# Last pair's first back attention: row sums taken by matmuls with a 0/1 pattern and the mix divided behind them

## The chip, the cores and the metric

The kernel runs on one core of one Trainium2 chip. The metric is the device time of one execution in microseconds (us). The kernel before takes 651.56 us, the median of three runs (649.15 to 652.43).

## The reference, cut to what matters

Eight sequences of 128 rows and width 128 go through four rounds of "x = x + attention(norm(x), context); x = x + feed-forward(norm(x))". The context of a sequence has 120 rows. The change touches the attention and the feed-forward of round 1 (named L1X and L1F in the kernel):

```
Qh, Kh, Vh = heads of x @ W_Q + b_Q, ctx @ W_K + b_K, ctx @ W_V + b_V     # 16 heads of width 8
scores     = einsum(Qh, Kh) / sqrt(8)  + causal, padded keys and rows at -inf
importances = nan_to_num(softmax(scores))
attn       = einsum('bhqk,bhkd->bhqd', importances, Vh)
x          = x + heads_joined(attn) @ W_O + b_O                            # L1X

Wq = sign(W / g) * min(round(|W / g|), 1),   g = mean(|W|) + 1e-6          # ternary weights of L1F
x  = x + layernorm(gelu(norm(x) @ Wq_fc.T)) @ Wq_proj.T                    # L1F
```

A softmax divides each row of exponentials by its sum. The quotient can be taken before the product with the values or after it: the sum belongs to one head and one query row.

## The kernel before

Two sequences make a pair, and the two sequences of a pair are the two lanes, 0 and 1; there are four pairs. A pair first goes through round 0 (the "early" steps, stream `p`, and the "front" steps, stream `f`, with 32 expert tiles of 8 products each) and then, lane by lane, through the six layers L1X to L3F (the "back" steps, streams `0` and `1`). Each engine writes its steps as four generators, and a table of letters, `ORDER`, says for each engine from which stream the next step is taken. An engine runs its instructions strictly in that order and waits at each for semaphores. The front of the next pair overlaps the back of the pair before it. The back of the last pair has no front beside it any more: from about 550 us on only its two lanes are left, and TensorE gets spare transposes of the identity (L688) in the slots where the table puts an `f`. At the beginning 14 warm steps of two dummy products (`keep_busy`) are spread in the same way.

All data is float32. One product of a 128x128 stationary tile (`lhsT`) is two MATMUL instructions in the trace; a transpose is one. TensorE writes three PSUM banks for each lane (`bank[lane][0..2]`, printed as bank10, bank11, bank12 for lane 1).

L1X of one lane goes like this. Four products give the scores of four heads each (128 rows by 4 times 120 columns), into three banks, the fourth into the first bank again. DVE reads each bank with the mask added (`take_scores`, recorded at L1502) and takes the row maxima (L1805). ACT computes the exponential head by head; `accum_out` makes each activation also deliver its row sum, by an extra instruction, ACTIVATION_READ_ACCUMULATOR (L1190). DVE inverts four sums at a time (`invert_sums`, L1816), POOL multiplies the four heads by them (`normalise_probs`, L1397), TensorE transposes the four heads (L785), and ACT or DVE copies the transposed bank to `wide_a` (`take_transposed`, or in the last pair `move_transposed` for the first `MOVED` = 2 banks, L1811). The mix then is 16 products, one for each head: a stationary tile of 32 columns of `v`, whose columns outside the head's own eight are zero, and 128 moving columns. Head 4j+c adds to the output partitions 32j to 32j+31:

```python
for c in range(4):
    for j in range(4):
        h = 4 * j + c
        last = mm(bank[lane][2][32 * j:32 * j + 32, 0:S], v[lane][0:K, 32 * h:32 * h + 32], ...)
```

So four instructions in a row go to four different groups of output partitions. ACT copies the mix (`mixT_ready`), TensorE multiplies it with `wo`, DVE adds it to x, and `turn_x` (L774) transposes the new x for L1F. In the program's order the lane whose L1X is first in the last pair is lane 1.

The ternary weights of L1F are made once, at the beginning, by DVE (`late_setup`, part of stream `0`): three small operations on the thresholds, then three operations of 512 columns for each of the two matrices, all in one step.

Of the kernel before, what the change touches and what calls it, by code (L numbers as in the profile page):

```python
# [23 lines left out]
MOVED = 2  # L24
# [23 lines left out]
    "PE": "pfppffpp00pp00fffffppppppppffffffffffffppff0fffppfpp00p00ffpfpf0pffpffppffffpffpfpfp0ffpfffpfffpfffp"  # L48
          "fffffpp0p10p01pfpff10fp10fff000f0p000f0010fp00f00f0p10ff001p10pff101101000f0pf0p1f1100101f0p11f10f11"
          "p0f001p10ff0ff10f11111111001ff1010110100fff1pfff1100p110101pfp1ff110f0ffffp0ffpff0pffpff11f01f1p01f1"  # L50
          "pf01ff1pf1f11011000fp011p00p11p100f1100p110f1p0101ff0p01ff10p000000001f1010111101000101fff10f01p1101"
          "0100ff01100ff1001011p1f110pf0110p1f01f01pff1000f100001f00p0ff00f001110f01100110f111f011f01f10001010f"
          "110100f01f10111110100101ff0f0f010f010111f10f01f1f11f11f1f110f110010110100f1ff1fffff1fff011ff11110011"
          "1001010001010010010000111000fff11101000000000101000001f111101f11100010001101111ff1110001101fffff",
    "Activation": "ppppp000ppppp0pppppp0ppppp00f0000pppf0ppfpffpfpfpfpppp00ppppp0p10ppp010f00011000p10f000001p10000fp10"
                  "0pp11f100100f001fp1111f0p1f11pp01p0110000001111101100001100000p1p0111p1111111ppp0101ff1111p000pf00pp"
                  "ff0f11pffp111111001110000p10p11p01p1101000p111pp10001p010000101111000p001000111000001110pp0001011f01"
                  "11111p11p0011p001f10000001101000pf00110001110101f0p111f11f001ff1100100110111110100010000000001111011"
                  "1100111111111101001100111100110101111110001000011100000111000100000110010010010111000010110101110101"
                  "1111010",  # L60
    "DVE": "ppppp0ppp0pppppppppppfffpfpfppppppfff00pppppfpfffppffffppffpffppppfpfffpppp0ffffpppppfffpppfffpppfpf"
           "ppf0ff1pff0f000f10fpff00011ffff101100000f1pp01pff000ffp0pp0p110p000ffffff0011101p001pppp11000000f11f"
           "f011f0pf11111f11f0ppfppppf01f10101101p001f01pppf00ffff1fffffpff00ppffp000f00fff111111011ffp1111111ff"
           "p11pffffp00f11p0000ff0111ppp1pp011p01ppp000f001ff10000f110p00f1111000p100101ppp0f0ppfpf11ff111101ff0"
           "0000010ffff1p0f111011110010000pf1f0011f111010pfff000011f0pp0001101101ff010f10010f0111000111ff1f11f00"
           "00000f0ff1110111111f11f000000fff1111111f10ff11001111110110110000100001111100000100100110100100000000"
           "01110000111110000001111110111100000011111110101",
    "Pool": "pppp1000f0fp111100000011f000011p1001110011000001011110101111fff1000p00001111111p01001101100011000011"
            "1000f10110111ff0000010011110000110111010010011010001011011111fff110110111000100111000010101000100011"
            "1011",  # L70
    "SP": "pppfffffffpffffffffffffffffpffffpffffffffffffffffffffpffffffffffffffffff0ppfff1ffffffffffffffpffffff"
          "fff0fffffffff1f1ff0pfffffffffffffffffpfffffffffff10ffff01f1001ffff",
}


def width(members):
    return sum(n for _, n in members)


def build(nc, x_in, ctx_in, q_mask, k_mask, pair_mask, packs, experts, gates_of, out):  # L80
    with ExitStack() as stack:
# [301 lines left out]
        with nc.Block() as block:  # L383
# [103 lines left out]
            def _(pe):  # L487
# [1600 lines left out]
```

## Time and profile before

| What | us |
| --- | --- |
| median of 3 runs | 651.56 |
| the profiled execution's own time | 650.43 |
| its span (first to last instruction) | 648.8 |
| TensorE (PE) busy | 629.2 |
| VectorE (DVE) busy | 504.2 |
| ScalarE (ACT) busy | 367.1 |
| GpSimd (POOL) busy | 212.4 |

The page also cuts the span into 40 slices: PE stands at 9 tenths or more nearly everywhere, with 8 tenths in the first slice and in several of the last seven. DMA moves little after about 550 us. The chain that ended last runs through PE for 88% of the span and through ACT for 5%. All times in the rows are counted from the start of the span. In a row of a timeline the first number is the start, the second the length, "xN" the instructions merged into the row, and the brackets give idle time before it and what ended it.

### The profile page before, as it was taken

The page shows a single profiled execution, that of the slowest core. Times are in us where ns is not written, and L with a number is a line of the kernel's source. Part 1 is how long each engine was busy: PE and PEld are TensorE (multiplying, and loading weights), DVE is VectorE, ACT ScalarE, POOL GpSimd, SP SyncE. Part 2 cuts the span into 40 slices and gives each one's busy share as a digit, 9 for nine tenths or more (in the row PEclk, how much of TensorE's full clock was granted, in tenths as well). Part 3 has the DMA queues.
Part 4 walks back from the last instruction along what each step waited for, and adds up shares of the span by engine and source line. Part 5 has one row for each costly group of instructions (what it writes and reads, how often), then busy time and mean ns, then how long its engine had stood idle before and what let it go on. Part 6 is the DMA issues. An engine that isn't in the chain of part 4 may idle for free.

```text
span 648.8 us, 14778 instructions
## 1 busy us (share of the span) xinstructions
PE 629.2 (97%) x5582; PEld 580.7 (90%) x5582; DVE 504.2 (78%) x1352; ACT 367.1 (57%) x1255; POOL 212.4 (33%) x252
## 2 busy tenths in 40 slices
PE   8999999899999999999999999999999999898889
PEld 7899999788999999999889999988899999567878
DVE  3886677898696868887987889879778586775776
ACT  3442132377465747354665677568666563866774
POOL 1000004465031512424531444154343531643040
DMA  8986969887614734899525318451552720000000
GB/s 339 413 285 217 308 215 330 295 281 255 238 38 131 260 123 134 293 302 349 169 90 175 103 47 289 162 193 35 162 202 98 268 74 5 6 2 1 2 2 9
DMA packets 37078, 111.93 MB, mean 173 GB/s; under 512 B 8976, under 2 KB 11664, under 8 KB 36496
## 3 DMA queue, kind: packets, MB, share of 16 engines
q1 hardware_dynamic: 37008, 110.99, 49.7%
q8 instruction: 44, 0.72, 0.4%
q14 instruction: 26, 0.21, 0.1%
HBM read 109.93 MB, written 1.05 MB: 171 GB/s over the span
## 4 chain that ended last, share of the span: by engine, by line
PE 88%; ACT 5%; DVE 4%; DMA 2%; issue 1%; POOL 0%; SPq 0%; DVEq 0%; ACTq 0%
PE bank L489 37%; PE e_bank L489 37%; PE p_bank L489 5%; PE bank L785 4%; ACT wide_b L1190 3%; DMA gated<-gates_of 2%; PE bank L774 1%; DVE gated L1499 1%; PE p_bank L594 1%; ACT wide_a L1045 1%; PE e_bank L688 1%; PE bank L1023 1%; PE bank L867 1%; DVE f_route L1499 0%; PE bank L627 0%
## 5 line engine op out<-in xcount | busy, mean ns | idle before, releaser
L489 PE MATMUL e_bank<-weights,gated 128*128 128x128 f32 x1984 | 235.2, 275 | 0.7 <-DVE gated L1499 0.7
L489 PEld LDWEIGHTS e_bank<-weights,gated 128*128 128x128 f32 x1984 | 228.2, 192 | 3.9 <-issue 1.6
L1190 ACT ACTIVATE wide_b<-wide_b,max_neg 128x120 f32<-128x120 f32 x272 | 103.4, 385 | 10.0 <-DVE max_neg L1805 6.2
L1397 POOL TENSOR_TENSOR wide_b<-wide_b,row_inv 128x480 f32<-128x480 f32 x64 | 70.9, 1114 | 115.1 <-DVE row_inv L1816 115.0
L1499 DVE TENSOR_TENSOR gated<-gated,f_v 128x1024 f32<-128x1024 f32 x64 | 77.2, 1234 | 9.1 <-DMA gated<-gates_of 5.0
L1389 POOL TENSOR_TENSOR rstd<-var_eps,w_const 128x1 f32<-128x1 f32 (+1 forms) x48 | 33.7, 702 | 152.9 <-DVE var_eps L1495 152.8
L1499 DVE TENSOR_TENSOR gated<-gated,f_xnT 128x1024 f32<-128x1024 f32 x60 | 77.8, 1333 | 2.8 <-DMA gated<-gates_of 2.6
L1045 ACT ACTIVATE wide_a<-bank 120x512 f32<-120x512 f32 (+5 forms) x103 | 53.5, 539 | 46.1 <-PE bank L489 19.0
L1190 ACT ACTIVATION_READ_ACCUMULATOR wide_b<-wide_b,max_neg 128x1 f32 x272 | 52.1, 191 | 0.0
L1805 DVE TENSOR_REDUCE max_neg<-wide_b 128x4 f32<-128x480 f32 x64 | 41.8, 653 | 2.2
L1045 ACT ACTIVATE f_v<-e_bank 128x512 f32<-128x512 f32 x32 | 19.2, 600 | 36.1 <-PE e_bank L489 36.1
L785 PE MATMUL bank<-w_const,wide_b 128*120 128x128 f32 x256 | 37.1, 275 | 2.4 <-POOL wide_b L1397 2.1
L1282 ACT ACTIVATE wide_a<-bank,w_L2f 128x128 f32<-128x128 f32 x128 | 34.7, 417 | 4.7 <-PE bank L489 4.7
L785 PEld LDWEIGHTS bank<-w_const,wide_b 128*120 128x120 f32 x256 | 28.8, 138 | 6.9 <-issue 4.9
L1045 ACT ACTIVATE wide_b<-bank 128x480 f32<-128x480 f32 (+2 forms) x40 | 20.6, 520 | 22.1 <-PE bank L489 22.1
L1343 POOL TENSOR_TENSOR f_rstd<-f_var_eps,w_const 128x2 f32<-128x2 f32 x8 | 8.4, 1045 | 73.0 <-DVE f_var_eps L1495 65.9
L489 PE MATMUL bank<-w_L2f,wide_a 128*128 128x128 f32 x256 | 31.4, 276 | 0.0
L489 PE MATMUL bank<-xnT,w_L2f 128*128 128x128 f32 x256 | 31.2, 276 | 0.0
L1095 ACT ACTIVATE f_b<-p_bank,f_max_neg 128x128 f32<-128x128 f32 x56 | 19.8, 371 | 19.6 <-DVE f_max_neg L1565 19.6
L489 PEld LDWEIGHTS bank<-w_L2f,wide_a 128*128 128x128 f32 x256 | 29.9, 192 | 0.4
L489 PEld LDWEIGHTS bank<-xnT,w_L2f 128*128 128x128 f32 x256 | 29.9, 193 | 0.0
L1502 DVE SCALAR_TENSOR_TENSOR wide_b<-bank,rstd,w_L3x 128x480 f32<-128x480 f32 x32 | 22.6, 706 | 7.6 <-PE bank L489 7.5
(274 smaller groups left out, 1236.8 us busy)
## 6 DMA issues: line engine op xcount, KB each, us to landing
gated<-gates_of SPq DMA_DIRECT2D x124, 512.0 KB, 5.6
weights<-in_experts SPq DMA_DIRECT2D x64, 512.0 KB, 6.1
w_L2f<-in_L2f SPq DMA_DIRECT2D x1, 2124.0 KB, 16.8
w_L3x<-in_L3x SPq DMA_DIRECT2D x1, 2108.0 KB, 11.9
w_L3f<-in_L3f SPq DMA_DIRECT2D x1, 1128.0 KB, 14.1
wide_b<-in_raw0f SPq DMA_DIRECT2D x1, 1024.0 KB, 7.5
w_L1f<-in_L1f SPq DMA_DIRECT2D x1, 516.0 KB, 8.0
x_next<-in_x SPq DMA_DIRECT2D x4, 128.0 KB, 4.6
```

What stands on the lines that cost most here:

```text
L489: return nc.tensor.matmul(o, lhsT, rhs, start=first, stop=last)
L785: last = nc.tensor.transpose(bank[lane][(1, 2, 0, 1)[i]][0:K, 128 * c:128 * c + 128], wide_b[lane][:, K * h:K * h + K], ident)
L1045: return nc.scalar.activation(o, i, ACT.Identity, bias=bias, scale=scale)
L1095: last = nc.scalar.activation(f_b[lane][:, 128 * h:128 * h + 128], unit_bank(pair, lane)[:, 128 * c:128 * c + 128], ACT.Exp, bias=f_max_ne ...
L1190: last = nc.scalar.activation(p, p, ACT.Exp, bias=max_neg[lane][:, h:h + 1], accum_out=row_sum[lane][:, h:h + 1])
L1282: last = nc.scalar.activation(wide_a[lane][:, at:at + 128], bank[lane][(1, 0, 2, 1)[i]][:, 128 * c:128 * c + 128], ACT.Gelu, bias=part["L2 ...
L1343: return nc.gpsimd.tensor_tensor(to[:, :], rows[:, :], part["const", "minus_half"][:, 0:2], ALU.pow)
L1389: nc.gpsimd.tensor_tensor(rstd[lane][:, cols], var_eps[lane][:, cols], part["const", "minus_half"][:, 0:cols.stop - cols.start], ALU.pow)\
L1397: nc.gpsimd.tensor_tensor(p3, p3, row_inv[lane][:, 4 * i:4 * i + 4].unsqueeze(2).broadcast_to([128, 4, K]), ALU.mult).then_inc(probs_norme ...
L1499: return nc.vector.tensor_tensor(o, a, c, op)
L1502: return nc.vector.scalar_tensor_tensor(o, a, scalar, c, op0, op1)
L1805: nc.vector.tensor_reduce(max_neg[lane][:, 4 * i:4 * i + 4], s3, AX.X, ALU.max, negate=True)\
```

## The change

In the last pair only, L1X no longer sums, inverts and multiplies ahead of the transposes. The exponentials run without `accum_out`. The transposes wait for the exponentials alone. For each group j of four heads, TensorE does four products with a 0/1 pattern (`head_cols`: 32 columns, ones in the head's eight) into columns 128 to 255 of the mix's bank, which gives every output partition the row sum of its head, and then the four products with `v`. The four groups are four steps; the third and the fourth wait for their own transposed bank. DVE then takes the reciprocal of 128x128 sums out of PSUM and multiplies the mix by it, which replaces ACT's copy. DVE moves one transposed bank (`MOVED_L1X` = 1) in place of two in L1X; ACT takes the other three. The step that makes the ternary weights is split into three, by two `yield`s. The first warm step of TensorE waits for the zeros it multiplies, as the early step did. And `ORDER` is new for all five engines.

```diff
-MOVED = 2
+MOVED_L1X, MOVED_L3X = 1, 2
...
 ORDER = {
-    "PE": "pfppffpp00pp00fffffppppppppffffffffffffppff0fffppfpp00p00ffpfpf0pffpffppffffpffpfpfp0ffpfffpfffpfffp"
...
+    "PE": "pfpffpffpfp0pp000fffpffpfpppppp0fffffffffpfpfffppfpp00p0ff0pfpfppffff0pffpffpf0fpfpfpffpffpffffpffff"
...
                 def front_steps():
+                    pe.wait_ge(idle_filled, 1)
                     for _ in range(WARM):
...
-                        pe.wait_ge(probs_normed[lane], probs_normed.upto(layer, i + 1, pair))
+                        if layer == L1X and pair == PAIRS - 1:
+                            pe.wait_ge(probs_ready[lane], probs_ready.upto(L1X, i + 1, pair))
+                        else:
+                            pe.wait_ge(probs_normed[lane], normed_upto(probs_normed, layer, i + 1, pair))
...
                     wait_turned(pe, lane, L1X, 1, pair)
-                    wait_turned(pe, lane, L1X, 3, pair)
-                    for c in range(4):
+                    if pair == PAIRS - 1:
                         for j in range(4):
-                            h = 4 * j + c
-                            last = mm(bank[lane][2][32 * j:32 * j + 32, 0:S], v[lane][0:K, 32 * h:32 * h + 32],
-                                      wide_a[lane][0:K, 128 * h:128 * h + 128], c == 0, c == 3)
+                            if j >= 2:
+                                wait_turned(pe, lane, L1X, j, pair)
+                            r = slice(32 * j, 32 * j + 32)
+                            for c in range(4):
+                                h = 4 * j + c
+                                mm(bank[lane][2][r, S:2 * S], part["const", "head_cols"][0:K, 32 * c:32 * c + 32],
+                                   wide_a[lane][0:K, 128 * h:128 * h + 128], c == 0, c == 3)
+                            for c in range(4):
+                                h = 4 * j + c
+                                last = mm(bank[lane][2][r, 0:S], v[lane][0:K, 32 * h:32 * h + 32],
+                                          wide_a[lane][0:K, 128 * h:128 * h + 128], c == 0, c == 3)
+                            if j < 3:
+                                yield
...
-                            last = nc.scalar.activation(p, p, ACT.Exp, bias=max_neg[lane][:, h:h + 1],
-                                                        accum_out=row_sum[lane][:, h:h + 1])
+                            if layer == L1X and pair == PAIRS - 1:
+                                last = nc.scalar.activation(p, p, ACT.Exp, bias=max_neg[lane][:, h:h + 1])
...
                     def normalise_probs(layer):
+                        if layer == L1X and pair == PAIRS - 1:
+                            return
...
                     link(ts(threshold[:, 0:2], threshold[:, 0:2], 0.5, None, ALU.mult))
+                    yield
...
+                        if late_sums:
+                            dve.wait_ge(mix_psum[lane], mix_psum.upto(L1X, 1, pair))
+                            link(nc.vector.reciprocal(wide_b[lane][:, S:2 * S], bank[lane][2][:, S:2 * S]))
+                            tt(wide_b[lane][:, 0:S], bank[lane][2][:, 0:S], wide_b[lane][:, S:2 * S], ALU.mult)\
+                                .then_inc(mixT_ready[lane], 1)
```

What the new table does is seen in the order of an engine's instructions. First TensorE, at the mix of lane 1 in the last pair; bank00 to bank02 are lane 0's banks, L688 is a spare transpose. Before:

```order
L785 MATMUL bank12<-w_const,wide_b_1 120x128 x4
L688 MATMUL e_bank<-w_const 128x128 x9
L489 MATMUL bank00<-wide_a_0,small_0 128x480
L785 MATMUL bank10<-w_const,wide_b_1 120x128 x4
L785 MATMUL bank11<-w_const,wide_b_1 120x128 x4
L688 MATMUL e_bank<-w_const 128x128 x6
L489 MATMUL bank12<-wide_a_1,v_1 32x128 x16
```

and in the changed kernel, down to the first of the four groups:

```order
L501 MATMUL bank02<-wide_a_0,small_0 128x480
L801 MATMUL bank12<-w_const,wide_b_1 120x128 x4
L801 MATMUL bank10<-w_const,wide_b_1 120x128 x4
L801 MATMUL bank11<-w_const,wide_b_1 120x128 x4
L501 MATMUL bank00<-wide_a_0,small_0 128x480
L501 MATMUL bank12<-wide_a_1,w_const 32x128 x4
L501 MATMUL bank12<-wide_a_1,v_1 32x128 x4
```

The spares between the transposes are gone, lane 0's fourth scores product stands directly ahead of the mix, and the last two rows stand four times in a row with nothing between them; lane 0's mix has the same form, right behind lane 1's product with the ternary `proj`.

Second DVE, around the normalised mix of lane 1 in the last pair; the rows with mask1_0 read lane 0's scores, the row with x_mid_bias1_1 makes lane 1's new x. Before:

```order
L1502 SCALAR_TENSOR_TENSOR wide_b_0<-bank02,mask1_0 128x480
L1805 TENSOR_REDUCE max_neg_0<-wide_b_0 128x4
L1816 RECIPROCAL row_inv_0<-row_sum_0 128x4
L1502 SCALAR_TENSOR_TENSOR wide_b_0<-bank00,mask1_0 128x480
L1502 SCALAR_TENSOR_TENSOR x_1<-bank10,row_ok_1,x_mid_bias1_1 128x128
```

and in the changed kernel:

```order
L1540 SCALAR_TENSOR_TENSOR wide_b_0<-bank02,mask1_0 128x480
L1845 TENSOR_REDUCE max_neg_0<-wide_b_0 128x4
L1879 RECIPROCAL wide_b_1<-bank12 128x128
L1537 TENSOR_TENSOR wide_b_1<-bank12,wide_b_1 128x128
L1540 SCALAR_TENSOR_TENSOR wide_b_0<-bank00,mask1_0 128x480
```

Lane 0's fourth bank of scores now stands behind the reciprocal, which waits for lane 1's whole mix.

Third DVE at the beginning, around the thresholds of the ternary weights; f_xn is the normalised x of the first pair. Before:

```order
L1495 TENSOR_SCALAR f_var_eps<-f_mean_var 128x2
L1496 TENSOR_SCALAR f_xn<-f_x0,f_mean_var,f_rstd 128x128 x2
L1496 TENSOR_SCALAR threshold<-bank00 128x2
L1495 TENSOR_SCALAR threshold<-threshold 128x2 x2
L1495 TENSOR_SCALAR wide_a_1<-w_L1f,threshold 128x512
```

and in the changed kernel:

```order
L1533 TENSOR_SCALAR f_var_eps<-f_mean_var 128x2
L1534 TENSOR_SCALAR threshold<-bank00 128x2
L1533 TENSOR_SCALAR threshold<-threshold 128x2 x2
L1534 TENSOR_SCALAR f_xn<-f_x0,f_mean_var,f_rstd 128x128 x2
L1533 TENSOR_SCALAR wide_a_1<-w_L1f,threshold 128x512
```

The three threshold operations moved ahead of f_xn, which waits for POOL. On TensorE the four products of w_L1f with wide_a_1 moved from behind the second expert tile to ahead of the first gate transposes, and eight of the twelve dummies that stood there moved to earlier slots.

## Rows read from the trace of the kernel before

**Rows 1.** Busy time by stretch: us, then PE, PEld, DVE, ACT, POOL; PEclk, DMA.

```profile
500.00:525.00 25.00, 25.00 (x252) 23.83 (x253) 16.68 (x36) 15.10 (x62) 10.47 (x12) 1.00 0.60 201
550.00:575.00 25.00, 21.86 (x191) 15.57 (x191) 18.00 (x47) 20.93 (x86) 16.21 (x18) 1.00 0.03 7
575.00:600.00 25.00, 21.67 (x151) 17.49 (x150) 15.85 (x72) 14.85 (x45) 7.94 (x10) 1.00 0.00 1
```

**Rows 2.** What PE waited for, 550 to 650 us: total, times, longest.

```profile
PE bank L785 <- POOL wide_b L1397: 2.1, 3, 1.6
```

**Rows 3.** PE timeline of L1X and L1F in the last pair.

```profile
561.66 0.97 PE L489 MATMUL bank<-wide_a,small 128*128 128x480 f32 x2
564.69 1.08 PE L489 MATMUL bank<-wide_a,v 120*32 120x128 f32 x32
565.70 0.48 PE L489 MATMUL bank<-w_L2x,ctx_back 128*120 128x128 f32 x2
567.52 0.27 PE L774 MATMUL bank<-w_const,x 128*128 128x128 f32 x1
573.31 1.08 PE L489 MATMUL bank<-wide_a,v 120*32 120x128 f32 x32
574.32 0.33 PE L879 MATMUL bank<-w_const,small 120*128 120x120 f32 x1
576.21 0.27 PE L774 MATMUL bank<-w_const,x 128*128 128x128 f32 x1
```

**Rows 4.** PE by tile shape, whole span: count, busy us, mean ns of one.

```profile
L489 PE MATMUL bank<-wide_a,v 120*32 120x128 f32 x256 | 8.5, 275 | 0.1
L489 PE MATMUL bank<-wide_a,v 120*64 120x128 f32 x256 | 17.5, 279 | 1.0 <-ACT wide_a L1045 0.7 <-DVE wide_a L1811 0.3
L489 PE MATMUL e_bank<-weights,gated 128*128 128x128 f32 x1984 | 235.2, 275 | 0.7 <-DVE gated L1499 0.7
```

**Rows 5.** ACT timeline in the last pair's L1X and L2F.

```profile
554.37 0.40 ACT L1190 ACTIVATE wide_b<-wide_b,max_neg 128x120 f32<-128x120 f32 x1 [0.66 <-DVE max_neg L1805]
554.77 0.38 ACT L1190 ACTIVATE wide_b<-wide_b,max_neg 128x120 f32<-128x120 f32 x1
563.46 1.08 ACT L1045 ACTIVATE wide_a<-bank 120x512 f32<-120x512 f32 x2
596.92 6.30 ACT L1282 ACTIVATE wide_a<-bank,w_L2f 128x128 f32<-128x128 f32 x24 [0.43 <-PE bank L489]
```

**Rows 6.** DVE groups by shape: count, busy us, mean ns of one.

```profile
L1603 DVE RECIPROCAL f_group<-f_group 128x16 f32<-128x16 f32 x8 | 2.0, 253 | 0.3
L1599 DVE RECIPROCAL f_group<-f_group 128x32 f32<-128x32 f32 x8 | 2.8, 353 | 0.3
L1499 DVE TENSOR_TENSOR x<-bank,x 128x128 f32<-128x128 f32 x16 | 4.6, 286 | 8.3 <-PE bank L489 8.0
```

**Rows 7.** DVE timeline: two banks of lane 1's scores in the last pair.

```profile
553.00 0.66 DVE L1502 SCALAR_TENSOR_TENSOR wide_b<-bank,mask 128x480 f32<-128x480 f32 x1 [0.89 <-PE bank L489]
554.26 0.65 DVE L1502 SCALAR_TENSOR_TENSOR wide_b<-bank,mask 128x480 f32<-128x480 f32 x1
```

**Rows 8.** DVE timeline at the beginning.

```profile
16.99 0.60 DVE L1496 TENSOR_SCALAR f_xn<-f_x,f_mean_var,f_rstd 128x128 f32<-128x128 f32 x2 [0.83 <-POOL f_rstd L1343]
17.51 0.15 DVE L1496 TENSOR_SCALAR threshold<-bank 128x2 f32<-128x2 f32 x1
18.10 0.48 DVE L1495 TENSOR_SCALAR wide_a<-w_L1f,threshold 128x512 f32<-128x512 f32 x1
27.59 0.29 DVE L1499 TENSOR_TENSOR f_gate<-f_route 128x128 f32<-128x128 f32 x1
```

**Rows 9.** PE timeline at the beginning.

```profile
25.57 2.84 PE L489 MATMUL e_bank<-small 128*128 128x128 f32 x24
28.25 1.47 PE L627 MATMUL bank<-w_const,f_gate 128*128 128x128 f32 x12
37.14 1.06 PE L489 MATMUL bank<-w_L1f,wide_a 128*128 128x128 f32 x8
```

More of the change, by code:

```diff
@@ L55 @@
[L55 to L67, printed above, removed]
@@ L819, in back_lane @@
                     wait_turned(pe, lane, L1X, 1, pair)
-                    wait_turned(pe, lane, L1X, 3, pair)
-                    for c in range(4):
+                    if pair == PAIRS - 1:
                         for j in range(4):
-                            h = 4 * j + c
-                            last = mm(bank[lane][2][32 * j:32 * j + 32, 0:S], v[lane][0:K, 32 * h:32 * h + 32],
-                                      wide_a[lane][0:K, 128 * h:128 * h + 128], c == 0, c == 3)
+                            if j >= 2:
[11 more added lines that the diff above has]
+                                yield
+                    else:
+                        wait_turned(pe, lane, L1X, 3, pair)
+                        for c in range(4):
+                            for j in range(4):
+                                h = 4 * j + c
+                                last = mm(bank[lane][2][32 * j:32 * j + 32, 0:S], v[lane][0:K, 32 * h:32 * h + 32],
+                                          wide_a[lane][0:K, 128 * h:128 * h + 128], c == 0, c == 3)
                     last.then_inc(mix_psum[lane], 1)
@@ L903, in back_lane @@
                     yield
-                    wait_turned(pe, lane, L2X, MOVED if pair == PAIRS - 1 else 0, pair)
+                    wait_turned(pe, lane, L2X, 0, pair)
                     for h in range(H2X):
@@ L1204, in softmax_banks @@
                                 yield
-                            if n >= behind and (pair < PAIRS - 1 or n - behind >= MOVED):
+                            if n >= behind and n - behind >= moved(layer, pair):
                                 take_transposed(layer, n - behind, lane)
@@ L1218, in back_lane @@
                     yield from softmax_banks(L1X, 2)
-                    act.wait_ge(mix_psum[lane], mix_psum.upto(L1X, 1, pair))
-                    copy(wide_b[lane][:, 0:S], bank[lane][2][:, 0:S]).then_inc(mixT_ready[lane], 1)
-                    yield
+                    if pair < PAIRS - 1:
+                        act.wait_ge(mix_psum[lane], mix_psum.upto(L1X, 1, pair))
+                        copy(wide_b[lane][:, 0:S], bank[lane][2][:, 0:S]).then_inc(mixT_ready[lane], 1)
+                        yield
                     act.wait_ge(kv_psum[lane], kv_psum.upto(L2X, 1, pair))
@@ L1727, in late_setup @@
                             link(last)
+                            yield
                     last.then_inc(setup_computed, 1)
@@ L1823, in softmax_banks @@
                             yield
-                        invert_sums(layer, 0, lane)
-                        yield
+                        late_sums = layer == L1X and pair == PAIRS - 1
+                        if not late_sums:
+                            invert_sums(layer, 0, lane)
+                            yield
                         take_scores(layer, 3, lane, scale, added)
@@ L1828, in softmax_banks @@
                         for i in range(1, 4):
-                            invert_sums(layer, i, lane)
-                            yield
-                            if pair == PAIRS - 1 and i <= MOVED:
+                            if not late_sums:
+                                invert_sums(layer, i, lane)
+                                yield
+                            if i <= moved(layer, pair):
                                 move_transposed(layer, i - 1, lane)
                                 yield
+                        if late_sums:
[3 more added lines that the diff above has]
+                                .then_inc(mixT_ready[lane], 1)
+                            yield
                     dve.wait_ge(kv_psum[lane], kv_psum.upto(L1X, 2, pair))
```

56 lines of the change are left out of this document (40 added, 16 removed).

## The prediction, made before the changed kernel ran

> **What bounds the kernel now.** I read the busy times by stretch first. In the middle of the span PE has no idle time (25.00 of 25.00 us from 500 to 525), so there only PE's own work counts. From 550 to 600, where the last pair's lanes run alone, PE is busy 21.86 and 21.67 of 25 and idles 6.5 us [rows 1]. The waits of PE in that stretch name POOL's normalised exponentials with 2.1 us in three waits [rows 2]; that is the wait the change removes. The PE timeline then shows the stage itself: lane 1's mix starts at 564.69, lane 1's new x is turned at 567.52, lane 0's mix starts at 573.31, lane 0's new x is turned at 576.21 [rows 3]. ACT runs exponentials nearly without a gap before the first mix, 0.40 us from one start to the next [rows 5]. So the stage is a chain over ACT, POOL and PE's order, and PE has some room in it.
>
> **The mix, the dear part.** The change adds 16 products for each lane and moves the order from "four output groups in turn" to "one group eight times". Three kinds of PE rows tell what that costs. Instructions with a stationary tile of 32 columns, issued in turn to four groups, take 8.5 us for 256, 33.2 ns each. Those of 64 columns, in turn to two groups, take 17.5/256 = 68.4 ns. Those over the full width take 235.2/1984 = 118.5 ns. The length of one alone is the same for all, 275 to 279 ns [rows 4]. The price goes as one over the number of groups that take turns: four instructions run beside each other, then two, then one. In the new order eight products, 16 instructions, in a row go to one group, so nothing can run beside them, and the next group's eight follow in program order. I cost them at 118.5 ns: 64 instructions for a lane, 7.6 us, where 32 now take 1.01 us (564.69 to 565.70, and 573.31 to 574.32) [rows 3]. The lower bound is 33.2 ns, 2.1 us, if the array overlaps them all the same; the upper is 4 x 33.2 = 133 or 2 x 68.4 = 137 ns, 8.8 us. I take the full-width row: it is the only one in which one group takes everything. The Trainium skill ("TensorE: Matmul & The Clock Gate", section "Measured speedup vs the span model") reports 2.38 times for three column groups, less than the ratio here (118.5/33.2 = 3.6 for four). By that page, scaled to four groups (3.2, an estimate), the 64 instructions would take 1.01 x 2 x 3.2 = 6.4 us, and the sum below would be 2.4 us lower.
>
> **Lane 1, term by term.** (a) The start of the mix. Gone from the chain are POOL's multiplication and, in ACT, the accumulator reads. DVE reads a bank of scores every 1.26 us (553.00, 554.26) [rows 7]. Without the read I cost an exponential at 0.26 us, from the 24 activations without a sum in 6.30 us [rows 5], so ACT's 16 take 4.2 us. The new order makes ACT copy two things of lane 0 first, which PE delivers only behind lane 1's fourth scores product; I put the first exponential 1.5 us after 554.37. Then 4.2, a copy of 0.2, and the first transposed bank, 0.54 (half of 1.08) [rows 5]: 560.8. Lane 0's fourth scores product, 0.8 us long, ends at about 560.5 by DVE's pace. The mix starts at about 561.0, 3.7 us earlier than now. The third and fourth bank are copied by 562, while the first two groups still run, so their separate waits cost nothing; nor do they gain anything. (b) The mix ends 7.6 us later in place of 1.0: +6.6. (c) Between its end and the turn of x are now 567.52 - 565.70 = 1.8 us. ACT's copy goes; DVE's reciprocal of 128x128 comes. Rows of 16 and 32 columns take 253 and 353 ns, 6.25 ns a column, so 353 + 96 x 6.25 = 0.95 us for 128; the multiplication is a row of 0.29 [rows 6]. Bounds: 0.35 (the longest row there is) and 1.4 (the same out of PSUM at half the speed). Behind the wait on DVE stands lane 0's fourth bank of scores, 1.26 us, and only then lane 1's new x; the product with `wo` hides under it. Landing and waits 0.3, 0.95 + 0.29, 1.26, the new x 0.35: 3.2, so +1.4. The Trainium skill ("VectorE: DVE Perf Modes", section "First, the fixed hardware budget") says that the reciprocal divides iteratively with a repeat count of 8. At 0.96 GHz that makes 1.07 us plus the fixed part, an estimate; by it the sum would be 0.3 higher for both lanes, and the rows' slope of 6.25 ns agrees better with 6 cycles. Together lane 1's x is turned at -3.7 + 6.6 + 1.4 = +4.3.
>
> **Lane 0.** From there to lane 0's mix PE's order is the same before and after, 5.8 us (567.52 to 573.31) [rows 3]. All four banks of lane 0 are ready by then, so again the whole 7.6 lies on PE's path: +6.6. From its end to the turn of lane 0's x: 2.3 in place of 1.9, +0.4. Lane 0 is late by 4.3 + 6.6 + 0.4 = 11.3. Lane 1 doesn't escape: its keys and its next x stand behind lane 0's mix on PE. What comes later has the same work in nearly the same order, and the two lanes wait for each other there; I let 0.8 be absorbed in PE's idle time of 575 to 600 [rows 1]. The tail: +10.5. Bounds: about 0 at 33 ns (below), +13 at 137 ns. The 32 inverted sums, the 8 multiplications on POOL and ACT's other savings are in (a) and count for nothing elsewhere.
>
> **The beginning.** The thresholds move into DVE's 0.83 us wait for POOL: 18.10 - 17.51 = 0.59 us off the chain to the first gates (27.59) [rows 8]. PE's dummies end at 28.25, 0.37 after f_gate is written at 27.88; eight of them move away. And eight instructions, 0.95 us, move from 37.14, where PE is full, to ahead of the gates, where only dummies ran [rows 9]. At best 0.6 + 0.4 + 0.9 = 1.9 us; nothing if the DMA-fed tiles behind can't keep up. I take 1.5, since PE has hardly any idle time from then to 550 that could eat it. The ternary step's division alone, and the wait for the zeros, cost nothing: DVE's and PE's rows around them keep their order. The rest of the table I cost at 0, within 1 us either way; two more table loads of ACT fall where PE is full.
>
> **The sum.** 650.4 (the profiled execution) + 10.5 - 1.5 = 659.4. That execution is 1.1 below the median of the runs, 651.56, so the median should be between 659.4 and 660.5; I say 660.
>
> **Rivals.** First, the groups run side by side after all. For it: the array is seen to run four of these tiles at once, and neighbouring groups touch at their borders. Against: the ladder of 33, 68 and 118 ns, which has no step left below one group. The mix then takes 64 x 33.2 = 2.1 us: lane 1 is -3.7 + 1.1 + 1.4 = -1.2, lane 0 +0.3, the tail about 0, and the beginning's 1.5 stays: 649, not slower. It decides from 48 ns an instruction down, where two mixes of 3.1 us use up what (a) and the beginning give. Second, half the added 13 us finds room: PE idles 6.5 us from 550 to 600 and ran spare transposes there besides. Then the tail is +5.3 and the time 654.2. Against it: the mix is one unbroken row in PE's order, and the other lane's work stands behind it. Third, PE's clock falls while the array is a quarter filled for 7.6 us. Granted was 1.00 in every stretch, which is 2.4 GHz [rows 1]; at the lower level, 1.2 GHz, the two mixes take 15 us more: 675.
>
> **How the numbers follow.** Less than 0.5% (3.3 us: under 648.3 faster, over 654.8 slower) can't be told from no change here. Forecast 0.75, all slower, with a range of its own of 655 to 665. Side by side 0.12, split between faster (0.07) and the same (0.05). Half hidden 0.10, 0.07 the same, 0.02 slower, 0.01 faster. Clock 0.03, slower. Faster 0.08, same 0.12, slower 0.80. The range 651 to 665 leaves out the first rival and the third.
>
> **What would show it.** Right: groups of 32-column products in the last pair with about 118 ns an instruction, 7 to 8 us for each lane without a gap; a DVE reciprocal of about 1 us in two places; lane 0's x turned near 586 (576.2 + 11.3 - 1.5); the first gate transposes near 27.4; and the busy time of PE up by 10 to 13 us. Wrong: the mix in 2 to 3 us; or the mix as long as said, but the turn of lane 0's x late by less than 6 us; or a granted clock under 1.

## The result, and the profile after

The changed kernel takes 661.03 us, the median of 4 runs (659.83 to 661.50), where the kernel before takes 651.99 beside it (649.15 to 653.44): a ratio of 1.0144, 95% interval 1.0125 to 1.0162. It is slower by 1.4%. Of the four executions the profiled one (659.83) shows a mean granted clock of 1.000 and the other three (660.71 to 661.50) 0.997, so sums over stages below go by traces and not by this median. The page of the changed kernel gives the span and PE's work; the span was 648.8 and PE 629.2 before.

```profile
span 658.2 us, 14857 instructions
...
PE 639.1 (97%) x5646; PEld 590.6 (90%) x5646; DVE 502.2 (76%) x1346; ACT 370.8 (56%) x1225; POOL 198.0 (30%) x244
```

PE is busy for 9.9 us longer, and the span is 9.4 us longer. The last two stretches of [rows 1], with the columns as there:

```profile
550.00:575.00 25.00, 20.97 (x146) 14.32 (x145) 15.71 (x35) 16.12 (x48) 8.74 (x11) 1.00 0.03 9
575.00:600.00 25.00, 22.82 (x180) 19.09 (x179) 13.01 (x53) 11.99 (x33) 4.14 (x7) 1.00 0.01 2
```

The granted clock is 1.00 in both. From 550 to 600 PE is busy for 43.8 us, about as before (43.5), but it got less far: the turn of lane 0's x, at 576.21 in [rows 3], comes at 585.54. PE's timeline, with the rows that answer to [rows 3] and the border between the first two groups of lane 1's mix in full:

```profile
549.91 0.27 PE L787 MATMUL bank<-w_const,xn_mid 128*128 128x128 f32 x1
...
560.56 0.62 PE L801 MATMUL bank<-w_const,wide_b 128*120 128x128 f32 x4 [0.29 <-ACT wide_b L1223]
561.02 0.97 PE L501 MATMUL bank<-wide_a,small 128*128 128x480 f32 x2
561.92 1.06 PE L501 MATMUL bank<-wide_a,w_const 120*32 120x128 f32 x8
562.82 0.71 PE L501 MATMUL bank<-wide_a,v 120*32 120x128 f32 x5
563.26 0.30 PE L501 MATMUL bank<-wide_a,w_const 120*32 120x128 f32 x1
563.37 0.27 PE L501 MATMUL bank<-wide_a,v 120*32 120x128 f32 x1
563.40 0.27 PE L501 MATMUL bank<-wide_a,w_const 120*32 120x128 f32 x1
563.48 0.27 PE L501 MATMUL bank<-wide_a,v 120*32 120x128 f32 x1
563.51 0.27 PE L501 MATMUL bank<-wide_a,w_const 120*32 120x128 f32 x1
563.59 0.27 PE L501 MATMUL bank<-wide_a,v 120*32 120x128 f32 x1
563.62 0.71 PE L501 MATMUL bank<-wide_a,w_const 120*32 120x128 f32 x5
...
567.81 0.48 PE L501 MATMUL bank<-w_L2x,ctx_back 128*120 128x128 f32 x2
...
570.76 0.33 PE L787 MATMUL bank<-w_const,x 128*128 128x128 f32 x1 [0.16 <-DVE x L1540]
...
576.96 1.06 PE L501 MATMUL bank<-wide_a,w_const 120*32 120x128 f32 x8
...
582.85 0.32 PE L911 MATMUL bank<-w_const,small 120*128 120x120 f32 x1
...
585.54 0.27 PE L787 MATMUL bank<-w_const,x 128*128 128x128 f32 x1
```

Read the starts. Lane 1's mix runs from 561.92 to 567.81 and lane 0's from 576.96 to 582.85, 5.89 us each for 64 instructions, 92 ns on average. Within a group eight start in 0.90 us (561.92 to 562.82), 112 ns apart: one alone, as forecast. The ninth, with which the group passes from its sums to its values and so to other columns of the bank, starts 0.11 us behind the eighth like the others, so it is not the adding into one place that keeps them apart. Whether it is the product itself or the load of its stationary tile stays open: PEld's timeline has the group's first eight loads end to end as well, in 0.79 us (561.92 to 562.71). At the border to another group it is different. The last three of the old group (`v`) and the first three of the new one (`w_const`) start in turn, six in 0.36 us (563.26 to 563.62). Three such borders in each mix give back 1.3 us of the 64 x 0.112 = 7.2. PE by tile shape shows the sum, to compare with [rows 4]: the 320 instructions of 32 columns now take 23.1 us, where 256 took 8.5.

```profile
L501 PE MATMUL bank<-wide_a,v 120*32 120x128 f32 x256 | 14.6, 275 | 0.0
L501 PE MATMUL bank<-wide_a,w_const 120*32 120x128 f32 x64 | 8.5, 276 | 0.0
```

DVE's timeline behind lane 1's mix, which answers to [rows 6] and to the order shown for DVE:

```profile
567.92 0.96 DVE L1879 RECIPROCAL wide_b<-bank 128x128 f32<-128x128 f32 x1 [4.72 <-PE bank L501]
568.91 0.29 DVE L1537 TENSOR_TENSOR wide_b<-bank,wide_b 128x128 f32<-128x128 f32 x1
569.12 0.65 DVE L1540 SCALAR_TENSOR_TENSOR wide_b<-bank,mask 128x480 f32<-128x480 f32 x1
...
570.37 0.34 DVE L1540 SCALAR_TENSOR_TENSOR x<-bank,row_ok,x_mid_bias 128x128 f32<-128x128 f32 x1
```

The reciprocal of 128x128 takes 0.96 us (0.95 forecast), and DVE waited 4.72 us for it. ACT's first eight exponentials of lane 1, to compare with [rows 5], and further on the four of lane 0's fourth bank with the two copies behind them; then, from the kernel before, the last of the 24 exponentials that start in one run at 554.37:

```profile
555.48 2.39 ACT L1223 ACTIVATE wide_b<-wide_b,max_neg 128x120 f32<-128x120 f32 x8
...
570.49 1.26 ACT L1223 ACTIVATE wide_b<-wide_b,max_neg 128x120 f32<-128x120 f32 x4 [1.24 <-DVE max_neg L1845]
571.65 0.58 ACT L1077 ACTIVATE v<-bank 120x512 f32<-120x512 f32 x1
572.12 0.26 ACT L1077 ACTIVATE xnT<-bank 128x128 f32<-128x128 f32 x1
```

```profile
563.09 0.39 ACT L1190 ACTIVATE wide_b<-wide_b,max_neg 128x120 f32<-128x120 f32 x1
```

Without the sum eight take 2.39 us, and what stands behind them starts 2.29 us after the first (557.77): one every 0.29 us. With it the first two start 0.40 us apart [rows 5], and over all 24 it is one every 0.38 us (8.72 us for 23 steps).

At the beginning the change did gain: the first gate transposes start at 27.96 (28.25 in [rows 9]), and the products of `w_L1f` behind them at 43.05, where they started at 44.23. But PE then waits in a place where it hardly did before. PE's row behind that wait, and DVE's timeline that explains it:

```profile
102.12 1.16 PE L501 MATMUL p_bank<-f_xnT,f_b 128*128 128x128 f32 x8 [1.68 <-ACT f_b L1127]
```

```profile
95.62 1.22 DVE L1537 TENSOR_TENSOR gated<-gated,f_v 128x1024 f32<-128x1024 f32 x1 [1.43 <-DMA gated<-gates_of]
98.69 1.23 DVE L1537 TENSOR_TENSOR gated<-gated,f_v 128x1024 f32<-128x1024 f32 x1 [1.85 <-DMA gated<-gates_of]
99.84 0.68 DVE L1603 TENSOR_REDUCE f_max_neg<-p_bank 128x4 f32<-128x512 f32 x1
```

The row maxima at 99.84, for which ACT's `f_b` and with it PE wait, stand behind multiplications that wait for gates from a DMA (1.43 and 1.85 us). Before, the same row stood two tiles earlier:

```profile
96.67 0.69 DVE L1565 TENSOR_REDUCE f_max_neg<-p_bank 128x4 f32<-128x512 f32 x1 [0.42 <-PE p_bank L489]
```

Of the gain 0.23 us is left when the last pair begins (549.91 in place of 550.14). That is one execution of each: the traces of later versions whose program is the same up to there, and whose clock stayed at 1.00, begin the last pair between 548.70 and 549.66, and one with the old beginning begins it at 552.63.

### The profile page after: what moved, and what is told of

Read it like the earlier page. It is cut to its first block, busy times and chain, and to the rows that moved or that the text cites. A ratio compares the mean times of both kernels' runs of the same rounds, so it can differ in the third digit from the quotient of the medians.

```text
span 658.2 us, 14857 instructions
## 1 busy us (share of the span) xinstructions
PE 639.1 (97%) x5646; PEld 590.6 (90%) x5646; DVE 502.2 (76%) x1346; ACT 370.8 (56%) x1225; POOL 198.0 (30%) x244
## 4 chain that ended last, share of the span: by engine, by line
PE 88%; ACT 5%; DMA 3%; DVE 3%; issue 1%; POOL 0%; SPq 0%; DVEq 0%
PE bank L501 38%; PE e_bank L501 35%; PE p_bank L501 5%; PE bank L801 4%; DMA gated<-gates_of 3%; ACT wide_b L1225 2%; PE bank L787 1%; PE e_bank L701 1%; ACT wide_b L1223 1%; PE p_bank L606 1%; PE bank L899 1%; DVE gated L1537 1%; DVE wide_b L1540 1%; PE bank L1055 1%; DVE max_neg L1845 1%
## 5 line engine op out<-in xcount | busy, mean ns | idle before, releaser
L1225 ACT ACTIVATE wide_b<-wide_b,max_neg 128x120 f32<-128x120 f32 x240 | 91.7, 388 | 16.0 <-DVE max_neg L1845 15.2
L1435 POOL TENSOR_TENSOR wide_b<-wide_b,row_inv 128x480 f32<-128x480 f32 x56 | 60.3, 1087 | 97.6 <-DVE row_inv L1856 97.6
L1425 POOL TENSOR_TENSOR rstd<-var_eps,w_const 128x1 f32<-128x1 f32 (+1 forms) x48 | 29.6, 618 | 171.0 <-DVE var_eps L1533 170.5
L1537 DVE TENSOR_TENSOR gated<-gated,f_xnT 128x1024 f32<-128x1024 f32 x60 | 75.5, 1298 | 6.3 <-DMA gated<-gates_of 6.1
L1225 ACT ACTIVATION_READ_ACCUMULATOR wide_b<-wide_b,max_neg 128x1 f32 x240 | 46.3, 193 | 0.0
L501 PE MATMUL bank<-wide_a,v 120*32 120x128 f32 (+1 forms) x512 | 32.1, 277 | 0.4 <-DVE wide_a L1851 0.3
L501 PEld LDWEIGHTS bank<-wide_a,v 120*32 120x32 f32 (+1 forms) x512 | 25.6, 123 | 5.0 <-issue 2.8
```

Of the source, the lines that this page charges most:

```text
L501: return nc.tensor.matmul(o, lhsT, rhs, start=first, stop=last)
L1225: last = nc.scalar.activation(p, p, ACT.Exp, bias=max_neg[lane][:, h:h + 1], accum_out=row_sum[lane][:, h:h + 1])
L1425: nc.gpsimd.tensor_tensor(rstd[lane][:, cols], var_eps[lane][:, cols], part["const", "minus_half"][:, 0:cols.stop - cols.start], ALU.pow)\
L1435: nc.gpsimd.tensor_tensor(p3, p3, row_inv[lane][:, 4 * i:4 * i + 4].unsqueeze(2).broadcast_to([128, 4, K]), ALU.mult).then_inc(probs_norme ...
L1537: return nc.vector.tensor_tensor(o, a, c, op)
```

## The experiments

The question was whether the added 9.4 us are the order of the mix, the division behind it, or the table, and where the beginning's gain went. Each ratio is against the kernel before, run beside it on the same chip. "The stage" is the time from the turn of lane 1's xn_mid to the turn of lane 0's x on PE: 26.07 us before (550.14 to 576.21), 35.63 in the changed kernel.

| Version | us | before | ratio, 95% interval |
| --- | --- | --- | --- |
| mix in turn | 651.97 | 651.22 | 1.0010 (0.9996 to 1.0025) |
| two groups in turn | 653.87 | 651.22 | 1.0042 (1.0028 to 1.0057) |
| kernel before, one group | 654.38 | 651.22 | 1.0047 (1.0031 to 1.0063) |
| bank first | 658.42 | 651.22 | 1.0116 (1.0093 to 1.0139) |
| turn and bank | 651.23 | 651.05 | 1.0003 (0.9983 to 1.0023) |
| and maxima earlier | 650.02 | 651.05 | 0.9971 (0.9956 to 0.9987) |
| turn, bank, sums first | 650.59 | 651.05 | 0.9996 (0.9978 to 1.0014) |
| beginning only | 650.57 | 651.05 | 0.9985 (0.9967 to 1.0003) |
| everything | 648.35 | 650.89 | 0.9958 (0.9945 to 0.9971) |
| beginning, maxima, old attention | 647.80 | 650.89 | 0.9950 (0.9934 to 0.9966) |

**The mix in turn over four groups.** In the last pair, in the changed kernel (shortened; the waits for the third and fourth transposed bank now stand ahead of all 64 instructions):

```diff
-    for j in range(4):
-        for c in range(4):  (pattern into group j)
-        for c in range(4):  (v into group j)
+    for c in range(4):
+        for j in range(4):  (pattern into group j)
+    for c in range(4):
+        for j in range(4):  (v into group j)
```

> The changed kernel with the same 64 instructions for a lane's mix, but in turn over the four output groups (first the 16 products with the pattern, then the 16 with v). Theory, the price of one group at a time: the mix falls from 5.89 us to 64 x 33.2 ns = 2.1 us, 3.8 us less for each lane, and both lie on the path: the turn of lane 0's x comes 7.6 us earlier (578.0), the span is 650.6 and the time 653.4. Rival one, the division behind the mix and its place in DVE's order are the loss: the mix is as short, but the turn of lane 0's x gains under 2 us and the time stays at 659 or more. Rival two, lane 1's mix lies beside other work: only lane 0's 3.8 us come back, time 657.

PE's timeline:

```profile
549.52 0.27 PE L787 MATMUL bank<-w_const,xn_mid 128*128 128x128 f32 x1
...
561.60 1.08 PE L501 MATMUL bank<-wide_a,w_const 120*32 120x128 f32 x32
...
563.49 0.48 PE L501 MATMUL bank<-w_L2x,ctx_back 128*120 128x128 f32 x2
...
573.12 1.08 PE L501 MATMUL bank<-wide_a,w_const 120*32 120x128 f32 x32 [0.40 <-ACT wide_a L1078]
...
575.01 0.32 PE L912 MATMUL bank<-w_const,small 120*128 120x120 f32 x1
...
577.72 0.27 PE L787 MATMUL bank<-w_const,x 128*128 128x128 f32 x1
```

Each mix takes 1.89 us (561.60 to 563.49), 29.5 ns an instruction, and the stage 28.20. The span is 650.4. The mix's order alone carries nearly the whole loss, and both lanes' mixes lie on the path: 8.0 us of mix came off, 7.4 of stage. Both rivals fall. The time is 1.4 us below the 653.4 expected, which was counted from the median of 661.03; counted from the profiled 659.83 it would have been 652.2.

**Two groups in turn.** The same edit, with groups 0 and 1 first and then 2 and 3.

> The changed kernel with two output groups in turn (0 and 1, then 2 and 3) in place of one. Theory, the price goes as one over the groups that take turns: 64 x 68.4 ns = 4.4 us by the row of 64-column tiles, less what the border between the halves gives back (0.3 to 0.5 us), so 3.9 to 4.4 us a mix, 1.5 to 2 us less than 5.89; two mixes give 3 to 4 us, time 657 to 658. Rival, two groups are still one queue: 5.9 us a mix, time 661. Third, they run like four: 2.1 us, time 653.4.

```profile
562.64 1.07 PE L501 MATMUL bank<-wide_a,w_const 120*32 120x128 f32 x16
...
565.86 0.48 PE L501 MATMUL bank<-w_L2x,ctx_back 128*120 128x128 f32 x2
```

3.22 us for lane 1's mix (562.64 to 565.86), 50 ns an instruction, and the stage 30.28 (550.65 to 580.93 for the two turns). That is better than the row of 64-column tiles promised: within a half 16 start in 0.90 us (562.64 to 563.54), 56 ns apart, half of 112, and the one border between the halves gives back its 0.4. So the price is 112 ns divided by the number of groups that take turns, less what the borders overlap. The stage follows the mix one to one: 5.34 us shorter in the two mixes, 5.35 in the stage. The time, 653.87, is 3 us below the 657 to 658 expected, of which the shorter mixes explain 1.4 to 2.4 (3.22 for 3.9 to 4.4, twice).

**The kernel before, one group after the other.** The loop over the 16 products is sorted by group in the last pair; nothing else is changed.

> The kernel before with one edit: in the last pair the 16 products of the mix run one output group after the other (no pattern products, no division behind, old order). Theory as predicted, 118.5 ns each: 32 x 118.5 = 3.8 us instead of 1.01, both lanes on the path, 652.0 + 5.6 = 657.6. Theory as the changed kernel shows it (110 ns inside a group, about 0.44 us given back at each of three borders): 32 x 110 - 1.3 = 2.2 us, 1.2 us more for each lane, time 654.4. Rival, the mix lies beside other work: 652.

```profile
567.17 2.43 PE L489 MATMUL bank<-wide_a,v 120*32 120x128 f32 x32
569.53 0.48 PE L489 MATMUL bank<-w_L2x,ctx_back 128*120 128x128 f32 x2
```

2.36 us where the mix took 1.01, and 3.1 us of time (0.47% of 651) for 2.7 us in the two mixes. The loss is there without the pattern, the division and the new table. The number with the borders counted (2.2) is near; the prediction's 118.5 ns (3.8) is too dear.

**Lane 0's fourth bank ahead of the division.** Two letters of DVE's row in the table are exchanged.

> The changed kernel with two neighbouring steps of DVE exchanged: lane 0's fourth bank of scores is read ahead of lane 1's division instead of behind it. The prediction's step (c) has those 1.26 us on the path to lane 1's new x: the turn of lane 1's x then comes 1.2 us earlier after the mix's end (1.7 in place of 2.95), and the time is 659.8. Rival: TensorE's own product for L3X (1.02 us from 569.58) stands ahead of that turn and ends at 570.6 anyhow, so the turn gains under 0.2 us and the time stays within 0.4 of 661.

Rows of PE (lane 1's mix ends with the first, x is turned with the second) and of ACT:

```profile
567.26 0.48 PE L501 MATMUL bank<-w_L2x,ctx_back 128*120 128x128 f32 x2
...
569.88 0.27 PE L787 MATMUL bank<-w_const,x 128*128 128x128 f32 x1
...
575.43 1.06 PE L501 MATMUL bank<-wide_a,w_const 120*32 120x128 f32 x8
```

```profile
568.59 1.24 ACT L1223 ACTIVATE wide_b<-wide_b,max_neg 128x120 f32<-128x120 f32 x4
...
570.58 0.27 ACT L1077 ACTIVATE xnT<-bank 128x128 f32<-128x128 f32 x1
```

From the mix's end to the turn it takes 2.62 us where it took 2.95: 0.33 less; the theory said 1.2, the rival under 0.2. Yet from there to lane 0's mix it is 5.55 in place of 6.20. ACT is the reason: the four exponentials of that bank ran at 570.49 in the changed kernel, ahead of the copies at 571.65 and 572.12, the second of which turns lane 1's x over to the next product; now they run at 568.59 and that copy at 570.58. The stage is 34.63, 1.00 shorter. The time fell by more than that (1.0116 for 1.0144, intervals that overlap), of which the stage explains 0.0015; the profiled execution also began its last pair 0.53 us earlier (549.38 for 549.91), where the two programs are the same. So the place in the order costs 1.0 us of the 1.26 put down, and two thirds of it behind the turn and over ACT.

**Turn and bank together.**

> The mix in turn and lane 0's fourth bank of scores read ahead of lane 1's division, both together. If the bank's place costs through ACT's order (its four exponentials stand ahead of the copies that lane 1 waits for), as the run with the bank alone showed with about 1.0 us from the turn of the first xn_mid to the turn of lane 0's x, the same stage falls from 28.2 to 27.2 us and the time from 652.0 to 651.0. If it cost only while DVE had long idled ahead of the division, nothing changes: 652.0.

The stage is 27.57 (548.70 to 576.27 for the two turns), 0.63 less than with the mix in turn alone, where 1.0 was expected; the times cannot tell these two apart.

**The row maxima earlier.** On top of that, one letter of DVE's row moves, at the beginning:

```diff
-    "DVE": "...ppppp0ffffpppp..."
+    "DVE": "...ppppp0ffpffppp..."
```

> The version with mix in turn and the bank first, and at the beginning one step of DVE two places earlier: the row maxima of the second gate half (at 99.84 us in the changed kernel) stand ahead of two multiplications that wait for gates from a DMA. Theory, the order on DVE costs the 1.68 us that PE waits at 102.1: the wait goes, lane 1's first step in the last pair comes 1.2 to 1.7 us earlier, time 649.5. Rival, the gates' transfers set the pace there (0.98 of the DMA engines' time is busy from 100 to 110 us): the wait returns behind it, time 651.0.

That is the place behind the same tile as before. PE now runs on into the product, with no wait in front, and the last pair begins at 548.04:

```profile
100.58 1.06 PE L501 MATMUL p_bank<-f_xnT,f_b 128*128 128x128 f32 x8
```

The wait is gone and the time 1.2 us less, with intervals that overlap a little. The same letter is all that parts two more pairs of versions in the table, "beginning only" from "beginning, maxima, old attention" (2.3 us) and "turn, bank, sums first" from "everything" (2.5 us), and there the intervals do not overlap. The rival falls: transfers set the pace of the gates, but PE did not wait for the gates, it waited for a row that stood behind them.

**The sums ahead of the values.** The pattern products write to the lane's first bank and signal for themselves; DVE takes the reciprocal while PE multiplies with `v`.

```diff
-    dve.wait_ge(mix_psum[lane], ...)
-    link(nc.vector.reciprocal(wide_b[lane][:, S:2 * S], bank[lane][2][:, S:2 * S]))
+    dve.wait_ge(idle_filled, 3 - lane)
+    link(nc.vector.reciprocal(wide_b[lane][:, S:2 * S], bank[lane][0][:, S:2 * S]))
+    dve.wait_ge(mix_psum[lane], ...)
```

> The version with mix in turn and the bank first; the sums go to the lane's first bank, with a signal of their own behind the 16 pattern products, so that DVE takes the reciprocal (0.96 us) while TensorE does the 16 products with v (0.9 us). Theory, the reciprocal lies whole on the path of both lanes: each gives back 0.9 us, the time is 649.2. Rival, lane 1's lies beside TensorE's own keys for L2X (1.0 us behind the mix) and its products for L3X: only lane 0's comes back, 650.1; or none, 651.0.

DVE's timeline, the two reciprocals:

```profile
564.10 0.95 DVE L1881 RECIPROCAL wide_b<-bank 128x128 f32<-128x128 f32 x1
...
573.83 0.96 DVE L1881 RECIPROCAL wide_b<-bank 128x128 f32<-128x128 f32 x1 [0.38 <-PE bank L501]
```

The stage is 26.73, 0.84 less than without it. Lane 1 gains nothing, since DVE is at lane 0's fourth bank and its maxima until 564.1 anyhow (the rival's result, by another cause); lane 0's reciprocal starts at 573.83, while PE is at its products with `v`, and all the gain is there. The time can't tell it from none.

**The beginning only.** The kernel before with the new table up to the last pair, the ternary step in three and the wait for the zeros.

> The kernel before with the beginning of the change alone: the ternary step in three, the wait for the zeros, and the new order table up to the last pair (about 550 us); behind it the old table and the old attention. The prediction's term for the beginning: -1.5 us, so 649.7 where the kernel before takes 651.2. By the trace of the changed kernel (first turn of the last pair 549.91 in place of 550.04) the gain is lost by 125 us: 651.1.

Inconclusive: 0.15% faster, 1 us, with an interval from 2.1 us faster to 0.2 slower, which holds both theories (the start of the last pair in the kernel before is 550.14 in the trace, not the 550.04 of the expectation). The profiled execution shows one thing that scatters such runs. PE's row behind the wait, and the granted clock after it:

```profile
102.47 1.78 PE L489 MATMUL p_bank<-f_xnT,f_b 128*128 128x128 f32 x8 [2.04 <-ACT f_b L1096]
```

```profile
104.00:106.00 2.00, 2.00 (x12) 2.00 (x11) 1.86 (x7) 0.23 (x1) 0.00 (x0) 0.50 1.01 412
```

After PE's 2.04 us without work the clock is at 0.50, the lower level of 1.2 GHz, from 104 to 106 us, and these eight instructions take 1.78 us where they take 1.16 in the changed kernel's trace. From their start to the next product with `f_b`, 64 instructions further on, it takes 9.77 us (to 112.24) where it took 8.14 (102.12 to 110.26): 1.6 us. In the changed kernel's trace the wait was 1.68 us and the clock stayed at 1.00; with the mix in turn it was 2.08 and the clock stayed at 1.00 too. So the wait alone does not decide it.

**Everything, and the old attention with the new beginning.** Two versions that the runs point to: all edits above together, and the beginning with the maxima earlier in front of the attention of before.

> The changed attention with everything that gave time together: mix in turn, lane 0's fourth bank of scores ahead of lane 1's division, reciprocal beside the products with v, and the row maxima of the second gate half two places earlier on DVE. If the gains add (the sums gave 0.84 us in the stage, the maxima 1.2 us of time, from 651.2), 649.2 where the kernel before takes 651.1; if the beginning's gain is lost again behind, 650.5.

> The beginning of the change with the row maxima two places earlier, and the attention of before: the mix in turn, normalised ahead of the transposes. From the run with the beginning alone (650.6) and the maxima's 1.2 us: 649.4. If the attention's new form is worth something once its mix runs in turn, this is slower than the version with everything together by up to 1 us; by the stages (26.1 us of before from the first turn to the turn of lane 0's x, 26.7 of the best form) it is the same or 0.6 us faster.

Both beat the kernel before, by 0.42% and 0.50%, and with it the changed one; their intervals overlap. The first expectation's 649.2 came out as 648.35, so the gains add at the least; the second's 649.4 came out as 647.80, and the version without the new attention is not the slower one. So the new table up to the last pair, with the beginning in it and one letter mended, is worth about 3 us, more than the 1.9 that the prediction gave the beginning at best; no run splits the rest of the table off. The new form of the attention is worth nothing measurable even at its best (stage 26.76 where the old one takes 26.07 to 26.08).

**The fourth scores product ahead of the last transposes.** Two letters of PE's row in the changed kernel are exchanged. There is one execution, 658.98 us, so only its trace counts.

> The changed kernel with one exchange in TensorE's order: lane 0's fourth scores product stands ahead of lane 1's last four transposes instead of behind them. What is read is the start of lane 1's mix after the turn of its xn_mid, 12.0 us in the changed kernel (561.92 - 549.91). If the product's 0.9 us behind the transposes are what held the mix, it starts 0.4 to 0.9 us sooner, 11.1 to 11.6 us after the turn, and the mix runs on into its fourth group without a gap, since the fourth bank's copy (0.5 us) lies beside the first three groups. Rival: the transposes are late by the product's length, the fourth group waits for its bank, and the mix ends where it did, 17.9 us after the turn.

```profile
549.51 0.27 PE L787 MATMUL bank<-w_const,xn_mid 128*128 128x128 f32 x1
...
561.10 1.06 PE L501 MATMUL bank<-wide_a,w_const 120*32 120x128 f32 x8
...
566.99 0.48 PE L501 MATMUL bank<-w_L2x,ctx_back 128*120 128x128 f32 x2
```

The mix starts 11.59 us after the turn in place of 12.01 and ends after 17.48 in place of 17.90, 0.42 less, at the low end of the expectation; the fourth group did not wait.

## Why the prediction was right, and which of its terms were off

The forecast of 660 is 1.0 below the 661.03 measured, and its likeliest case is the one that happened. The reason given, groups that no longer take turns, is shown by three runs that change that order, two in the changed kernel and one in the kernel before. Its terms, by the two traces (one execution each):

| Term | predicted | measured |
| --- | --- | --- |
| (a) start of lane 1's mix, after the turn of xn_mid | -3.7 | -2.54 |
| (b) lane 1's mix | +6.6 | +4.88 |
| (c) from its end to the turn of x | +1.4 | +1.13 |
| from there to lane 0's mix | 0 | +0.41 |
| lane 0's mix | +6.6 | +4.88 |
| from its end to the turn of lane 0's x | +0.4 | +0.80 |
| behind that | -0.8 | +0.07 |
| the beginning | -1.5 | -0.23 |
| sum | +9.0 | +9.4 |

The sum is right because errors of opposite sign met; the steps are to be judged one by one. Of the signs named ahead, lane 0's turn (585.54, near 586 said), the reciprocals of 0.96 us and PE's added work (9.9 us, 10 to 13 said) came; the mixes were shorter than the 7 to 8 us said, and the first gate transposes later (27.96, not 27.4).

(b) was mis-sized. The row chosen, 118.5 ns, was close to what one group alone costs (112), but the text let "the next group's eight follow in program order". They do not wait for it: the borders overlap, and 64 instructions take 5.89 us and not 7.6. The prediction had named those borders only for its first rival. That is 3.4 us too much over both lanes. The 6.4 us that the prediction worked out, as an estimate, from the Trainium skill ("TensorE: Matmul & The Clock Gate", section "Measured speedup vs the span model") are nearer, but not for its reason: in turn, four groups run 112/29.5 = 3.8 times as fast as one here, not 3.2.

(a) was too hopeful by 1.2 us. An exponential without its sum takes 0.29 us, not the 0.26 of the rows it was costed by, so 16 take 0.4 more. And the fourth scores product of lane 0, put at DVE's pace, stands in PE's order behind lane 1's last transposes (561.02, right behind 560.56); moved ahead of them it gives 0.42 back. The rest, about 0.4, no run splits.

(c) named the right parts and sizes for the reciprocal (0.96 for 0.95; the rows' slope of 6.25 ns a column holds). The 1.07 us and more that the prediction worked out, as an estimate, from the Trainium skill ("VectorE: DVE Perf Modes", section "First, the fixed hardware budget") are too long: the trace has 0.96. The place of the 1.26 us was wrong: PE's own product for L3X, 569.58 to 570.6, covers most of them before the turn, and they come back behind it through ACT. Behind lane 0's mix the reciprocal lies on the path: +0.80 for +0.4, and the run with the sums first gives 0.84 back there.

The absorbed 0.8 us did not exist: from the turn of lane 0's x to the end it takes 72.66 us, and took 72.59; in the traces of all the versions it is 72.55 to 72.73. PE's idle time there is that of a chain, which starts later and ends later.

The beginning is off by 1.3 us in these two traces; by the times (1.0 us for the beginning only, interval 2.1 to -0.2) the forecast 1.5 is not refuted, so what failed for certain is its argument and not its size. That argument, that PE has hardly any idle time from there to 550 that could eat the gain, looked only at the waits that were there. The new table put the row maxima of the second gate half behind two multiplications that wait for transfers, and made a wait where there had been none. The gates' transfers had been named as the risk; the order on DVE behind them had not. What the wait costs is shown by the runs with the maxima earlier: 1.2 to 2.5 us.

Of the rivals, side by side is refuted in its size but not in its mechanism: neighbouring groups do touch at their borders, with 1.3 us of 7.2. Half hidden is refuted by the run with two groups, where the stage gives back all that the mix does. The clock did not fall in the mix: 1.00 while a quarter of the array works. Two prices in the prediction do not follow from their own words, and nothing hung on them: half of the 13 us of mixes is 6.6, which leaves a tail of 3.9 and a time of 652.8 and not 654.2 (that is half the tail), and the reciprocal at half the speed would take about 1.75 us (0.15 and 128 x 12.5 ns) and not 1.4.

## What to carry to other kernels

Where small stationary tiles go to different groups of output partitions, count the price of an instruction as that of one alone divided by the groups that take turns, and let the innermost loop run over the groups; an order by group is a choice only if its earlier start is worth more. When a change moves steps in an order, look not only at the waits that it takes away but at each moved step's new neighbour ahead of it on the same engine: what that one waits for, the moved step now waits for too. And a gain near the beginning is worth only what is left behind the next wait on the way, the change's own new ones included.

## What the runs showed of the hardware that was not expected

- TensorE starts products of two groups in turn where one group's run ends and the next begins: three instructions of each, 0.36 us for six, with the later group's first instruction starting (563.26) ahead of the earlier group's sixth (563.37), by the records.
- One group alone takes 112 ns an instruction of 32 columns and 128 moving rows, two in turn 56, four in turn 29.5 to 33.
- Taking the row sums along costs ACT 0.09 us an exponential of 128x120: one every 0.38 us with them, one every 0.29 us without.
- Behind the same wait of TensorE the granted clock was 0.50 and 0.53 from 104 to 106 us in two traces (the beginning only, wait 2.04 us; two groups in turn, 1.89 us) and stayed at 1.00 in others (1.68 and 2.08 us); where it fell, the next 72 instructions took 1.6 us longer. Whether it also explains the rest of the scatter between executions of one kernel is not shown.
